# Layer-1 projections put into two stages, 8-bit float rows rounded in the matmul unit, and a bias moved into the attention, in a four-layer gated network

## The reference, cut to what matters

```python
# layer 1 attention: queries, keys and values rounded to 8-bit integers times a step
q = (layernorm(x) @ Wq + bq) * scale        # step per row and head of 32
kv = ctx @ Wkv + bkv                        # k: step per row and head; v: step per column over all 2048 rows
s = max(abs(t)) / 127; t = round(t / s) * s
# layer 2 attention
delta = rs * (attention(...) @ Wo.T + bo)
x += gate * ((delta - mean) / sqrt(var + eps) * ln_gamma + ln_beta)
# layer 2 feed-forward: rows as 8-bit floats with one scale for the whole tensor
h = layernorm(x); scale_x = max(abs(h)) / 448
x8 = (h / scale_x).astype(float8_e4m3fn)    # then x8 @ w8.T
```

## Time and profile before

| | us |
|---|---|
| median of 3 runs | 3229.5 (3224.81 to 3231.89) |
| profiled execution | 3235.41 |
| its span | 3233.5 |
| PE, DVE, ACT, POOL busy | 2633.2, 2484.8, 1907.9, 602.9 |

### The profile page before, as it was taken

How to read it: one execution, slowest core, us unless ns; L and a number is a source line. 1 busy time by engine, 2 the same in 40 slices (tenths; PEclk the granted TensorE clock), 3 DMA queues, 4 the chain that set the end, 5 groups by cost and what they waited for, 6 DMA issues and landing times. The chain is left out here.

```text
span 3233.5 us, 61058 instructions
## 1 busy us (share of the span) xinstructions
PE 2633.2 (81%) x21148; PEld 1373.5 (42%) x21148; DVE 2484.8 (77%) x4757; ACT 1907.9 (59%) x2773; POOL 602.9 (19%) x539
## 2 busy tenths in 40 slices
PE   4868999776799999999999678979789737759973
PEld 3434444333366565656566344434211213225542
DVE  5746667575699999999999469964599797975547
ACT  2555433233199999999999345532578335825541
POOL 4331000022100101001010515531011530030013
PEclk8987999897899999999999889989899868869996
DMA  4442431200100000000000020020332010042201
GB/s 156 148 173 86 149 117 53 101 1 13 23 8 7 14 7 14 7 9 12 7 8 0 17 92 1 1 95 1 79 78 54 23 52 1 1 121 47 44 8 56
DMA packets 65252, 152.12 MB, mean 47 GB/s; under 512 B 11744, under 2 KB 19952, under 8 KB 63280
## 3 DMA queue, kind: packets, MB, share of 16 engines
q1 hardware_dynamic: 62272, 140.43, 14.5%
q0 software_dynamic: 2800, 9.18, 0.9%
HBM read 93.61 MB, written 24.38 MB: 36 GB/s over the span
## 5 line engine op out<-in xcount | busy, mean ns | idle before, releaser
L1617 DVE TENSOR_REDUCE s_top<-ps 128x1 f32<-128x512 f32 x1024 | 656.8, 683 | 31.8 <-PE ps L1512 31.5
L1586 ACT ACTIVATE s_prob<-ps,s_shift,m_sq 128x1024 int16<-128x1024 f32 x512 | 615.2, 1202 | 30.9 <-DVE s_shift L1625 30.9
L1512 PE MATMUL ps<-s_ks,s_qs 128*128 128x512 f16 x1024 | 352.1, 386 | 61.6 <-issue 15.2
L1517 PEld LDWEIGHTS ps<-ident,s_prob 128*128 128x128 f16 x4096 | 272.3, 98 | 123.2 <-DVE m_o L1635 52.8
L1517 PE MATMUL ps<-ident,s_prob 128*128 128x128 f16 x4096 | 313.9, 220 | 0.7 <-ACT s_prob L1586 0.5
L1505 PE MATMUL ps<-s_ks,s_qs 128*128 128x512 f16 x1024 | 306.7, 381 | 0.8 <-ACT s_prob L1586 0.5
L1592 ACT ACTIVATE s_probT<-ps 128x1024 f16<-128x1024 int16 x256 | 262.1, 1024 | 5.4 <-PE ps L1517 5.0
L1008 PE MATMUL ps<-m_hT,m_w 128*128 128x512 f16 x1024 | 231.8, 381 | 1.9 <-PEq L105 1.9
L2435 DVE TENSOR_SCALAR s_prob<-ps,s_cap 128x1024 f32<-128x1024 f32 x128 | 158.2, 1269 | 25.1 <-PE ps L2344 25.1
L1630 DVE CAST s_probT<-ps 128x1024 f16<-128x1024 int16 x256 | 174.2, 680 | 2.9 <-PE ps L1517 2.8
L3058 DVE TENSOR_REDUCE s_ntop<-ps 128x1 f32<-128x512 f32 (+3 forms) x256 | 107.4, 483 | 87.1 <-PE ps L2918 87.1
(11 more groups left out here) (418 smaller groups left out, 5611.1 us busy)
## 6 DMA issues: line engine op xcount, KB each, us to landing
s_qs<-m_qT SPq DMA_DIRECT2D x144, 128.0 KB, 2.8
s_ks<-m_kT SPq DMA_DIRECT2D x96, 128.0 KB
numbers<-s_numbers SPq DMA_DIRECT2D x21, 512.0 KB, 2.8
s_slabs<-numbers SPq DMA_DIRECT2D x21, 512.0 KB, 6.2
m_ks<-context_parts SPq DMA_DIRECT2D x12, 512.0 KB
expert_rows<-s_y SPq DMA_DIRECT2D x19, 256.0 KB, 2.0
s_rows_in<-in_ctx SPq DMA_DIRECT2D x16, 256.0 KB, 3.3
x_sb<-in_L_ffn_W_up SPq DMA_DIRECT2D x4, 1024.0 KB, 7.2
```

The source lines that it names most:

```text
L1512: pe.matmul(quarter_at(q), qs[:, hb, bass.ds(t * P, P)], ks[:, hb, cols(q, 512)], start=True, stop=True).then_inc(s.top_scored, 1)
L1517: j = pe.transpose(turned(half, F16)[:, cols(m, P)], prob[:, u, cols(8 * half + m, P)].bitcast(F16), k.ident[:])
L1586: act.activation(prob[:, u, cols(half, HALF)], pair(half).rearrange("p m n -> p (m n)"), ACT.Exp, bias=shift[:, u:u + 1], scale=sq[:, bass ...
L1617: dve.tensor_reduce(top4[:, u, q:q + 1], quarter_at(q), AX.X, ALU.max).then_inc(s.top_read, 1)
```

## The change

Line numbers below are those of the kernel before; the new code's are given where an order is shown.

1. Layer 1, keys and values: `split_weights`, `quantised_heads` and `quantised_values` become one stage, `quantised_context`. The key columns of `Wkv` are loaded in four pieces ahead of the context, the value columns behind it. PE projects four tiles of keys ahead, then alternates a key tile, a group of values and the turn of an earlier tile. POOL now makes the low part of the value weights. ACT makes the value weights' high parts and waits for POOL's low parts before it splits the first tile of keys.
2. Layer 1, queries: `split_weights`, `transposed_parts` and `quantised_heads` become one stage, `quantised_queries`; tiles of `x` are normalised four ahead of their rounding, and the turned parts are copied out by ACT instead of DVE.
3. Layer 2: the gated beta is loaded, multiplied and added to `x` by POOL within `attention_clipped`; `project_normalise_add` loses it.
4. `fp8_rows`: ACT normalises each tile once and keeps it; DVE takes the maximum from it. The rounding is done by writes in 8-bit float: near values (`small`, by ACT), the half of the value (`half`) and the half clipped at 120 (`kept`), which PE adds with factors 1, 2 and -2 as it turns them (12 matmuls a tile instead of 4 transposes).

```diff
-            split_weights(k, k.i.L1_xattn_Wkv, wkv, context=cT)
-            quantised_heads(k, cT, wkv[:, :, :, 0:D], k.i.L1_xattn_bkv[0:D], 1.0, parts=kT, context=True)
-            quantised_values(k, cT, wkv, k.i.L1_xattn_bkv[D:2 * D], values, sv)
+            quantised_context(k, cT, k.i.L1_xattn_Wkv, k.i.L1_xattn_bkv, wkv, kT, values, sv)
...
-            split_weights(k, k.i.L1_xattn_Wq, wq)
-            transposed_parts(k, hT, taken=True)
-            quantised_heads(k, hT, wq, k.i.L1_xattn_bq, scale, sq=sq[:].rearrange("p (h t) -> p t h", t=T), ints=qT)
+            quantised_queries(k, hT, k.i.L1_xattn_Wq, k.i.L1_xattn_bq, scale, wq, sq[:].rearrange("p (h t) -> p t h", t=T), qT)
...
+def quantised_context(k, cT, w_in, bias, w, kT, values, sv):
+    AHEAD, RING = 4, 3
...
+        def _(pe):
+            pe.wait_ge(k.context_first, 16 * k.context_loads)
+            pe.wait_ge(s.w_lo, DC)
+            for t in range(AHEAD):
+                project(t)      
+                if t >= 2:
+                    turn(t - 2) 
+            pe.wait_ge(k.context_rest, 16 * k.context_loads)
+            pe.wait_ge(s.w_lo_v, DC)
+            for n in range(DC * G):
+                if n + AHEAD < T:
+                    project(n + AHEAD)
+                group(n)
+                if n + AHEAD - 2 < T:
+                    turn(n + AHEAD - 2)
+                if n >= 6 and n % 4 in (2, 3):
+                    turn_values(2 * (n // 4 - 1) + n % 4 - 2)
@@ quantised_context, vector @@
+            for t in range(T):
+                heads(t)
+                if t >= 8 and t % 4 == 0:
+                    value_numbers(t // 4 - 2)
+            value_numbers(DC - 2)
+            value_numbers(DC - 1)
@@ quantised_context, scalar @@
+            act.wait_ge(s.wv_loaded, 16)
+            for c in range(DC):
+                act.activation(w[:, 0, c, D:2 * D], nat[:, 1, c, :], ACT.Copy).then_inc(s.w_hi_v, 1)
+            act.wait_ge(s.bv_loaded, 16)
+            act.wait_ge(s.w_lo_v, DC)
+            for t in range(AHEAD - 2):
+                hi(t)
...
+def quantised_queries(k, hT, w_in, bias, scale, w, sq, ints):
@@ quantised_queries, tensor @@
+            for t in range(T + 2):
+                if t + 2 < T:
+                    turn_h(t + 2)
+                if t < T:
+                    project(t)
+                if t >= 2:
+                    turn(t - 2)
@@ quantised_queries, vector @@
+            for t in range(T):
+                if t + R < T:
+                    normal(t + R)
+                heads(t)
@@ attention_clipped, gpsimd @@
     def _(pool):
             pool.memset(ones[:], 1.0).then_inc(s.ones_ready, 1)
+            pool.wait_ge(s.beta_loaded, 16)
+            pool.tensor_tensor(beta[:], beta[:], k.gate[:, gate:gate + 1].broadcast_to([P, D]), ALU.mult).then_inc(s.beta_ready, 1)
+            pool.wait_ge(s.beta_ready, 1)
             for i in range(H // 4 * B):
                 c, b = i // B, i % B
+                pool.tensor_tensor(k.x[:, i, :], k.x[:, i, :], beta[:], ALU.add)
                 pool.wait_ge(s.inverted, i + 1)
@@ project_normalise_add, gpsimd @@
             for t in range(T):
-                pool.tensor_tensor(k.x[:, t, :], k.x[:, t, :], beta[:], ALU.add).then_inc(s.beta_added, 1)
                 pool.wait_ge(s.var_ready, t + 1)
@@ fp8_rows, scalar @@
+            for t in range(T):
+                act.wait_ge(s.offset_ready, t // R + 1)
+                act.activation(normal[:, t, :], k.x[:, t, :], ACT.Identity, bias=offset[:, t:t + 1],
+                               scale=k.rstd[:, t:t + 1]).then_inc(s.normal_ready, 1)
             copy_weights(k, s, act, weights, weight_banks(weights, 0, 1))
@@ fp8_rows, vector @@
+            for t in range(T):
+                dve.tensor_scalar(near[:, u, :], normal[:, t, :], edge[:, 0:1], edge[:, 1:2], ALU.min, ALU.max
+                                  ).then_inc(s.clipped, 1)
+                dve.tensor_scalar(half[:, u, :], normal[:, t, :], inv[:, 0:1], 0.5, ALU.mult, ALU.mult, saturate=False
+                                  ).then_inc(s.half_ready, 1)
+                dve.wait_ge(s.half_ready, t + 1)
+                dve.tensor_scalar(kept[:, u, :], half[:, u, :], 120.0, -120.0, ALU.min, ALU.max, saturate=False
+                                  ).then_inc(s.kept_ready, 1)
@@ fp8_rows, tensor @@
+                for c in range(DC):
+                    for m, part in enumerate((small, half, kept)):
+                        j = pe.matmul(k.ps[:, u, cols(c, P)], part[:, u, cols(c, P)], ident[:, m, :],
+                                      start=(m == 0), stop=(m == 2))
```

More of the change, by code:

```diff
@@ L1265, in _, with turn @@
[L1265 to L1275, removed]
+            def turn(t):
+                pe.wait_ge(s.numbers_ready, t + 1)
+                if t >= 2:
+                    pe.wait_ge(s.copied, t - 1)
+                for c in range(DC):
+                    i = pe.transpose(k.ps16[:, 2 + t % 2, cols(c, P)], numbers[:, t % 2, cols(c, P)], k.ident[:])
+                i.then_inc(s.turned, 1)
@@ L1279, in _ @@
             v = Steps(dve, s.vsteps)
-            dve.wait_ge(s.bias_loaded, 16)
[L1281 to L1307, removed]
-                                          scaled[:, u, :].rearrange("p (h d) -> p h d", d=HD),
-                                          step[:, u, :].unsqueeze(2).broadcast_to([P, H, HD]),
-                                          ALU.mult).then_inc(s.rows_ready, 1)
@@ L2303, in attention_clipped @@
         ones = s.sb("ones", [P, HD], F32)
+        beta = s.sb("beta", [P, D], F32)
         mask_i = s.sb("mask_i", [P, T], I32)
@@ L2638, in _ @@
             pe.matmul(k.ps[:, 3, 0:P], wide_top[:], k.ident32[:], start=True, stop=True).then_inc(s.total_ready, 1)
-            with pe.Fori(0, T // R) as i:
-                for u in range(R):
-                    pe.wait_ge(s.numbers_ready, R * i + u + 1)
-                    pe.wait_ge(s.copied, R * i + u + 1)
-                    for c in range(DC):
-                        j = pe.transpose(k.ps16[:, u, cols(c, P)], numbers[:, u, cols(c, P)], k.ident[:])
-                    j.then_inc(s.turned, 1)
+            pe.wait_ge(s.inv_ready, 1)
@@ L2659, in fp8_ffn @@
+            for t in range(T):
+                act.wait_ge(s.clipped, t + 1)
+                if t >= R:
+                    act.wait_ge(s.turned, t - R + 1)
+                act.activation(small[:, t % R, :], near[:, t % R, :], ACT.Copy, scale=inv[:, 0:1], saturate=False
+                               ).then_inc(s.small_ready, 1)
+                if t >= 2:
+                    copy_out(t - 2)
+            copy_out(T - 2)
+            copy_out(T - 1)
 def fp8_ffn(k, xT, wfc, wproj, sx, sfc, sproj, gate):
```

441 lines of the change are left out of this document (278 added, 163 removed).

## The result

The changed kernel takes **3171.0 us** (median of 4 runs, 3165.4 to 3173.8), the kernel before beside it 3230.7 (4 runs, 3224.8 to 3232.7): ratio 0.9813, 95% interval 0.9802 to 0.9825. The forecast was 3176, in a range from 3162 to 3197. The profiled execution took 3173.64, its span is 3171.7 against 3233.5 before, 61.8 less; the sum had said 54.

The account below looks back on a forecast made before the run. No engine was busy over 81%, so four barrier-closed stretches were each priced by their pacing engine. 21.7 + 12 + 12.2 − 1.8 + 10 = 54 us; from the profiled 3235.4, adjusted to the median 3229.5, the forecast was 3176, range 3162 to 3197.

Parts of the forecast that it names:

- Keys and values: Layer 1's merged keys and values stage: 146.9 to 125.3 us, PE pacing rounds of 5.63; gain 21.7, bounds 16 and 25.
- ahead of PE: 9.0: Start of keys and values: 2.25 MB must arrive before PE starts, 9.0 us into the stage.
- ACT's queue order is fixed: Keys and values: argument, with bytes needing 20 us, against ACT's wait for the value columns being hidden.
- Queries: Layer 1's merged queries stage: 99.6 to 87.8 us, DVE pacing; gain 12, bounds 4 and 16.
- 3.48 each: Queries: DVE's time per tile in the kernel before, taken as the base for 16 tiles before normalising and port meetings.
- Normalised projection: Layer 2's projection without beta: 63.2 to 50.9 us, PE becoming the pace; gain 12.2, bounds 9 and 13.
- Beta in the attention: Clipped attention: 1.8 us lost, by a load issue of about 0.5 and a last addition of 1.26; bounds 0.5 and 3.
- 8-bit rows: The 8-bit rows' stage: 73.0 to 62.9 us, late weight copies losing 8, rounding 1.35 a tile; gain 10, bounds 4 and 13.
- lockstep rival: Keys and queries: each round needs its own tile's whole chain, 10 us a key round, 8 a query tile; 3304, chance 0.03.
- ports and pace: Rival: POOL's port use costs queries 9, DVE-bound keys 3, 8-bit tiles at 1.85 cost 8; 3196, chance 0.15.
- no gain: Rival, whole kernel: another wait (context's second part, weight copies) gives all back; 3229, chance 0.01.
- better than the sum: Rival: ACT's wait hides, PE stays at high clock in the rounding, port meetings miss; 66 gained, 3163, chance 0.12.

Follow-up runs that it names:

- values_last: Changed kernel, with ACT and POOL taking the first two key tiles before the value weights in the keys' and values' stage: 3168.1 us, ratio 0.9804 to the kernel before.
- queries_no_low: Changed kernel, with POOL subtracting one column instead of 512 for the queries' low halves from the fourth tile on: 3168.8 us, ratio 0.981 to the kernel before.
- copies_split: Changed kernel, 8-bit rows: ACT copies 8 of 16 weight banks ahead of the normalised tiles, PE spreads the maximum after the twelfth bank: 3165.0 us, 0.9793 to before.
- undo_beta: Changed kernel with beta scaled and added in the normalised projection again, as in the kernel before: 3183.1 us, ratio 0.9852 to the kernel before.

## Why the prediction was right, and where its steps were off

- **Keys and values** (21.7 forecast, 17.4). The mechanism and the pace are exact: 5.63 a round. The step that failed is "ahead of PE: 9.0", sized by the rate of the kernel before for 2.25 MB: it measured 12.3, and the value columns' 20 measured 23.1. Between these and the first turn the working wrote 7.6 (27.6 less 20), though its terms add up to 7.0; 7.5 was measured. Steady rounds so begin 2.8 us late, and 1.5 were lost at the end: from DVE's last write to the barrier it took 5.2, not 3.7, and the last turn of values waits 1.2 of it for the copy of the turn before. What I called fixed ("ACT's queue order is fixed") was the right thing to look at, but undoing it alone gave 2.8 (values_last), since the value weights' low halves are the next late thing.
- **Queries** (12 forecast, 18.5). The meeting cost was right: 0.39 a tile, taken away by queries_no_low. The first tile met no subtraction, though (its step size took 0.18), which is 0.4 less. Mis-sized were the bare tile, "3.48 each": the last tiles, which meet nothing, come 3.29 apart, 0.2 less for each of 16; and the first bias addition, at 16.9 us and not 18.3, of which 1.0 is PE's first tile (4.26 and not 5.3). The end was 0.7 shorter too. Why the bare tile is shorter was not isolated: the steps are written out now instead of run in a loop with register counts, and the copy of the step size stands later among them.
- **Ports.** The Trainium skill ("SBUF — State Buffer", "Who interferes with whom") lets the one that issues first keep the shared ports for its whole instruction. The rows agree: DVE's step size is done 0.04 after POOL's instruction ends, so the price goes by what is left of that instruction: 0.39 of 1.15, and 0.07 when POOL starts 0.33 earlier. The same section says that a reduction never meets POOL here, and L1223 takes 0.69 beside it. My reading that the rule would cost 9 us more was wrong: it is a rule on who waits, not on how much of an instruction is left.
- **Normalised projection** (12.2, 11.8). Right: PE became the pace, with 118 matmuls in a row without a pause, 2.6 us for twelve:

```profile
2534.74 25.63 PE L2640 MATMUL ps<-m_wT,m_qT 128*128 128x512 f16 x118
```

- **Beta in the attention** (−1.8, −3.3). Both places were named; both were too small. The issue took 1.02 and not 0.5, and moved the first scores by 1.1; the last inversion waits 1.5 longer, not 1.26; the rest was not found.
- **8-bit rows** (10, 12.8). The loss by the copies was foreseen, with 8: copies_split gets 8.2 back. Smaller by 2 was the path to the maximum, at 36.6 and not 38.7, since copies queue at 0.92 and PE spreads at once; a tile took 1.31 and not 1.35. It is DVE's pace: the tiles keep it when PE's clock rises (0.56 over the first 6 us of the rounding, 1.00 from 12 us on).
- **Left out**: what the stage leaves behind. With the 192 matmuls of the rounding PE enters the next block at the high clock in eleven of twelve profiled executions, with the old rounding in none of two, and the third maximum comes 2.1 us earlier than in the kernel before. A term for the stage behind was missing; 1.0 of the 3.1 us gained there was not found.

The lockstep rival is refuted by 5.63 and 4.14 a tile, "ports and pace" by the same two and by 1.31 in the rounding, "no gain" by the time. Of what "better than the sum" asked for, ACT's wait did not hide (8.8 us of idle PE) and the meetings did not miss (0.39 a tile); PE did reach the high clock in the rounding, which did not change DVE's pace there. The 5 us below 3176 come from the mis-sized terms and the one left out.

## What to carry to other kernels

When stages are merged, write down for each in-order engine what its queue does while it waits for the first load or statistic: both holes found here (9 us on DVE, 9 on PE) were work that stood behind a later arrival, and moving eight copies into ACT's idle time gave back 8.2 us. After each such move ask which operation is late next, and which engine's ports it uses; two tries on the keys' hole of 8.8 us gave back 2.8 and 5.4. And price a meeting on the ports by what is left of the other's instruction: shifting one short step by its length removed most of it here (0.07 of 0.39 left).

## What the runs showed of the hardware that I had not expected

- PE's clock at the start of a stretch is not settled by the code ahead of it. In the normalised projection two profiled executions of the twelve with its new code had the high level in the first 6 us (PEclk 1.00, stretch 49.8), the ten others the low one at first (0.67 to 0.77, 51.1 to 51.5). In the two the clock had already risen in the transposes before (0.80 in the last 3 us ahead of the barrier, 0.50 in the ten). In the 8-bit block undo_beta had 0.63 where the changed kernel had 1.00, behind the same matmuls and the same pause. Such an edge is worth 1.6 to 1.7 us here.
- What a meeting with POOL costs DVE depends on when DVE's step comes. Beside the four subtractions of values_last three steps running took 0.8 to 0.9 longer each; a single subtraction in the same profile took 1.0 from the step that began 0.04 behind it, against the 0.39 in the queries:

```profile
655.72 1.16 POOL L1371 TENSOR_TENSOR s_f<-s_rows,s_f 128x512 f16<-128x512 f32 x1 [0.79 <-ACT s_f L1379]
```

```profile
655.76 1.66 DVE L1229 TENSOR_TENSOR s_scaled<-s_rows,s_inv 128x512 f32<-128x512 f32 x1
```

- The long stretch of unchanged code wandered from 1418.9 to 1429.2 us, more than any one order was worth. Some of it is in layer 1's attention, where every third group of heads came 58.4 to 61.4 us after the one before and the two others always 55.2 to 55.3, and some in layer 2's projections (160.1 to 164.9). Its cause was not looked for; it hides a gain of 3 us from the medians.
